# Two graph-attention layers and a binary layer: cross-partition maxima by transfers, last rows a window earlier, sign products one mix piece later, and a longer early tail

## The reference

```
def gat_layer(x, W, adj):
    Wh, Ws = split(x @ W, 2)
    a = softmax(Wh @ Ws.T) * adj
    return leaky_relu(a @ Wh + x, 0.01)

y = gat_layer(gat_layer(x, W_stack[0], adj), W_stack[1], adj)
x = layernorm(x + y)
xw = max(sign(x), 0) @ sign(weight).T
x = layernorm(x + relu(adj @ xw))
```

## Time and profile before

| | us |
|---|---|
| median of 3 runs (2173.22 to 2178.22) | 2175.34 |
| the profiled execution | 2172.28 |
| its span, first to last instruction | 2170.5 |
| TensorE busy | 2112.5 |
| VectorE, ScalarE, GpSimd busy | 1594.1, 908.4, 691.0 |
| granted TensorE clock, mean share | 0.996 |

### The profile page before, as it was taken

How to read it: one execution, slowest core, us unless ns; L and a number is a source line. 1 busy time by engine, 2 the same in 40 slices (tenths; PEclk the granted TensorE clock), 3 DMA queues, 4 the chain that set the end, 5 groups by cost and what they waited for, 6 DMA issues and landing times.

```text
span 2170.5 us, 38687 instructions
## 1 busy us (share of the span) xinstructions
PE 2112.5 (97%) x13260; PEld 1295.4 (60%) x13260; DVE 1594.1 (73%) x4051; ACT 908.4 (42%) x2043; POOL 691.0 (32%) x625
## 2 busy tenths in 40 slices
PE   6999999999999999999998999999999999999998
PEld 2446666666666666664445666666666666665444
DVE  7977877778777778777984676776677776766464
ACT  5764444434444444444764444344443444443000
POOL 2852223223223233323862332333323332332000
PEclk9999999999999999999999999999999999999999
DMA  7997878777877788779997978878978888779883
GB/s 217 213 216 153 174 156 169 146 158 153 165 151 167 153 164 158 160 149 231 213 215 143 186 157 167 169 159 170 173 155 163 169 169 173 159 147 236 237 275 118
DMA packets 779094, 380.11 MB, mean 175 GB/s; under 512 B 642576, under 2 KB 700944, under 8 KB 777232
## 3 DMA queue, kind: packets, MB, share of 16 engines
q1 hardware_dynamic: 768080, 341.82, 72.9%
q0 software_dynamic: 3328, 22.16, 6.9%
q10 hardware_dynamic: 7488, 13.63, 1.8%
HBM read 206.18 MB, written 59.11 MB: 122 GB/s over the span
## 4 chain that ended last, share of the span: by engine, by line
PE 85%; DVE 5%; issue 3%; DMA 3%; SPq 1%; ACT 1%; POOL 1%; DVEq 0%; POOLq 0%; ACTq 0%
PE banks L1120 35%; PE banks L1090 30%; PE banks L753 10%; PE banks L1615 6%; PE banks L1099 2%; DMA bits_t_a<-bits_a 1%; DMA adj_rows_a<-adj_rows 1%; PE banks L1079 1%; DVE halves_a L1345 1%; PE banks L584 1%; SPq L972 1%; POOL row_a L1281 0%; DVE acc_a L1367 0%; DVE work_a L1397 0%; DVE row_a L1300 0%
## 5 line engine op out<-in xcount | busy, mean ns | idle before, releaser
L1120 PE MATMUL banks<-values,probs_t_a 128*128 128x512 f16 x4056 | 959.1, 379 | 0.6 <-DVE acc_a L1367 0.6
L1281 POOL TENSOR_TENSOR row_a<-row_a,adj_rows_a 128x512 f32<-128x512 f32 (+1 forms) x364 | 456.7, 1269 | 1163.4 <-ACT row_a L1205 1126.0
L1120 PEld LDWEIGHTS banks<-values,probs_t_a 128*128 128x128 f16 x4056 | 397.1, 98 | 378.2 <-issue 2.4
L1090 PE MATMUL banks<-keys_t,q_even_a 128*128 128x256 f16 x3528 | 433.0, 273 | 12.8 <-ACT row_a L1197 10.2
L1345 DVE SCALAR_TENSOR_TENSOR halves_a<-row_a,halves_a 128x512 f16<-128x512 f32 (+1 forms) x364 | 277.5, 762 | 220.9 <-ACT halves_a L1220 218.3
L1197 ACT ACTIVATE row_a<-banks 128x256 f32<-128x256 f32 x468 | 177.3, 379 | 612.6 <-PE banks L1090 596.1
L1090 PEld LDWEIGHTS banks<-keys_t,q_even_a 128*128 128x128 f16 x3528 | 344.5, 98 | 114.5 <-ACT row_a L1197 9.3
L1090 PE MATMUL banks<-keys_t,q_odd_a 128*128 128x256 f16 x3024 | 370.0, 273 | 7.5 <-ACT row_a L1197 4.6
L1090 PEld LDWEIGHTS banks<-keys_t,q_odd_a 128*128 128x128 f16 x3024 | 294.1, 98 | 95.5 <-ACT row_a L1197 7.6
L1205 ACT ACTIVATE row_a<-row_a,shift_a,scales 128x512 f32<-128x512 f32 (+1 forms) x364 | 281.2, 774 | 161.7 <-DVE shift_a L1335 161.5
L1367 DVE SCALAR_TENSOR_TENSOR acc_a<-acc_a,factor_a,banks 128x512 f32<-128x512 f32 x312 | 232.8, 746 | 97.0 <-PE banks L1120 91.8
(11 more groups left out here) (130 smaller groups left out, 1479.2 us busy)
## 6 DMA issues: line engine op xcount, KB each, us to landing
adj_rows_a<-adj_rows SPq DMA_DIRECT2D x312, 256.0 KB, 3.2
adj_t<-adj_blocks POOLq DMA_DIRECT2D x104, 208.0 KB, 3.9
keys_t<-adj_t SPq DMA_DIRECT2D x26, 832.0 KB, 7.0
x_rows_a<-x_rows SPq DMA_DIRECT2D x52, 256.0 KB, 3.5
s_rows<-sum_rows_p SPq DMA_DIRECT2D x24, 512.0 KB, 3.1
values<-x_rows SPq DMA_DIRECT2D x13, 512.0 KB, 6.1
adj_rows_a<-adj_rows SPq DMA_DIRECT2D x52, 128.0 KB, 2.7
x_mid<-x_rows_a SPq DMA_DIRECT2D x26, 256.0 KB, 3.3
```

Source lines behind the costliest of these rows:

```text
L1090: last = pe.matmul(bank(w, name), queries(pair_of(w), q_block, qh, c), keys_t[:, kh, k_block, c, cols], start=(first and c == 0 and n == 0 ...
L1120: last = pe.matmul(out_bank(u), probs_t[:, turned_slot(w), u, ph * tiles + j, :], values[:, 4 * step_of(w) + j, vh, :], start=(j == 0 and ...
L1281: pool.tensor_tensor(piece, piece, adj_rows[:, n % ADJ_RING, 0:width(w)], ALU.mult).then_inc(masked, 1)
```

## The change

It has six parts. (1) `spread_w_peak` of layer 1's W is replaced by three functions: SP stores the 128 maxima to DRAM (`send_w_peak`), fetches them back broadcast to all partitions (`fetch_w_peaks`), and VectorE takes the maximum (`join_w_peaks`). The first all-reduce of W in layer 0 and those of the norms stay. (2) `spread_low_bits` becomes `gather_low_bits` on SP and a reduction in `note_low_bits`. (3) `last_rows` is cut into 16 parts of 3 matmuls, spread over windows 0 to 2 by a table. (4) Sign products stand behind mix (0,0), those of tiles 22 and 23 behind mix (1,1); `keep_product` stands behind the exponentials. (5) Six output banks, five early tiles. (6) In layer 0's start, W is scaled and split in two halves of columns, and the order of loads and turns is another.

```diff
-LAST_ROWS = 1
+LAST_ROWS = ((0, 1, 2, 3, 4), (4, 6, 7, 9, 10), (10, 12, 13, 15, 16))
-    LOADS_AHEAD = 8
+    LOADS_AHEAD = 11
...
+    def send_w_peak(sp):
+        sp.wait_ge(w_peak, layer + 1)
+        sp.dma_start(peak_row[:], facts[:, 0:1]).then_inc(w_peak_out, 16)
+    def fetch_w_peaks(sp):
+        sp.wait_ge(w_peak_out, 16)
...
+        sp.dma_start(w_peaks[:], peak_row.partition_broadcast(P)).then_inc(w_peak_in, 16)
+    def join_w_peaks(dve):
+        dve.wait_ge(w_peak_in, 16)
+        dve.reduce_max(facts[:, 1:2], w_peaks[:], AX_X).then_inc(w_peak_all, 1)
...
-    def last_rows(pe, t, side, part):
-        if part == 0:
+    def last_rows(pe, k):
+        t, side, c = T - 2 + k // 8, k // 4 % 2, k % 4
+        if c == 0:
             pe.wait_ge(turn_sem(t), landed_turn(t))
             pe.wait_ge(rows_copied, 4 * (first_pair + last_pair - 1 + side) if t == T - 2
                        else 4 * (first_pair + last_pair) + 1 + side)
...
     def sp_program(sp, turn_first_queries):       # project, layer 0
...
-            for i in range(1, LOADS_AHEAD):
+            load_x(sp, 1)
+            turn_x(sp, 0)
+            load_x(sp, 2)
+            turn_x(sp, 1)
+            for i in range(3, LOADS_AHEAD):
                 load_x(sp, i)
-            for t in range(RING):
-                turn_x(sp, t)
-                for i in range(LOADS_AHEAD + 2 * t, min(LOADS_AHEAD + 2 * t + 2, J)):
-                    load_x(sp, i)
+            turn_x(sp, 2)
+            for i in range(LOADS_AHEAD, J):
+                load_x(sp, i)
+            turn_x(sp, 3)
...
-            for c in range(DC):                   # act, layer 0
-                halve_w(c)
+            for side in (0, 1):
+                for c in range(DC):
+                    halve_w(c, cols_of(side))
...
             see_w(1)                              # dve, layer 0
-            x_lo_half(dve, 1)
             see_w(2)
             see_w(3)
             peak_of_pieces(dve)
+            x_lo_half(dve, 1)
             scale_w(dve)
-            for c in range(DC):
-                lo_w(c)
+            for side in (0, 1):
+                for c in range(DC):
+                    lo_w(c, side)
...
             for c in range(DC):                   # make_rows
-                if t == 0 and side == 0:
-                    pe.wait_ge(w_split, c + 1 if layer == 0 else DC + PIECES)
+                if t == 0 and layer == 0:
+                    pe.wait_ge(w_split, DC * side + c + 1)
+                elif t == 0 and side == 0:
+                    pe.wait_ge(w_split, 2 * DC + PIECES)
...
+            if ahead and piece_windows.get(w - 3, -1) == pieces - 1:      # attend, sp
+                ahead["send_w_peak"](sp)
+            if ahead and piece_windows.get(w - 5, -1) == pieces - 1:
+                ahead["fetch_w_peaks"](sp)
+            if last_layer and w == 5:
+                binary["gather_low_bits"](sp)
...
-            if LAST_ROWS <= w + LAG < LAST_ROWS + 2:                      # mix
-                now["last_rows"](pe, T - 2 + w + LAG - LAST_ROWS, u, piece)
+            if w + LAG < LAG:
+                for k in range(*LAST_ROWS[w + LAG][2 * u + piece:2 * u + piece + 2]):
+                    now["last_rows"](pe, k)
...
+            mix(w - LAG, 0, 0)                                            # attend, pe
             for t, u in made_now:
                 if t < binary["made_here"]:
                     pe.wait_ge(accumulated, through(w - LAG - 1, 1))
-                sign_product(pe, t)
-            mix(w - LAG, 0, 0)
+                    sign_product(pe, t)
...
             mix(w - LAG, 1, 1)
+            for t, u in made_now:
+                if t >= binary["made_here"]:
+                    sign_product(pe, t)
...
             copy_scores(w, 0)                                             # attend, act
-            for t, u in late_tiles(w, 7, 8) if last_layer else ():
-                keep_product(t)
             if 0 <= w - 1 < windows:
                 exps(w - 1)
+            if last_layer and w < windows:
+                for t, u in late_tiles(w, 7, 8):
+                    keep_product(t)
             copy_scores(w, 1)
...
-            if LAST_ROWS <= w < LAST_ROWS + 2:
-                now["copy_rows"](act, T - 2 + w - LAST_ROWS, 0)
+            if w == 2:
+                now["copy_rows"](act, T - 1, 0)
...
-            if LAST_ROWS <= w < LAST_ROWS + 2:
-                now["copy_rows"](act, T - 2 + w - LAST_ROWS, 1)
+            if w < LAG:
+                now["copy_rows"](act, T - 2 + w // 2, (w + 1) // 2)
...
+            if last_layer and w >= windows:
+                for t, u in late_tiles(w, 7, 8):
+                    keep_product(t)
...
-            if last_layer and w == 3:                                     # attend, pool
-                binary["spread_low_bits"](pool)
...
-            if ahead and piece_windows.get(w - 2, -1) == pieces - 1:
-                ahead["spread_w_peak"](pool)
...
-            if last_layer and w == 5:                                     # attend, dve
+            if last_layer and w == 8:
                 binary["note_low_bits"](dve)
...
-                if piece_windows.get(w - 3, -1) == pieces - 1:
+                if piece_windows.get(w - 7, -1) == pieces - 1:
+                    ahead["join_w_peaks"](dve)
                     ahead["scale_w"](dve)
...
-ADJ16_RING, OUT_RING, EARLY_TILES = 8, 4, 4
+ADJ16_RING, OUT_RING, EARLY_TILES = 8, 6, 5
...
+    def gather_low_bits(sp):
+        sp.wait_ge(low_bits_found, 1)
...
+        sp.dma_start(low_row[0:1], flag[:, 0:1]).then_inc(low_bits_gathered, 16)
     def note_low_bits(dve):
+        dve.wait_ge(low_bits_gathered, 16)
+        dve.reduce_max(flag[0:1, 1:2], low_row[0:1], AX_X).then_inc(low_bits_max, 1)
...
         for t in range(EARLY_TILES):                                      # binary, pe
             pe.wait_ge(adj16_loaded[t], 16)
+            if t == 4:
+                pe.wait_ge(accumulated, units)
             add_products(t, range(T - 2))
-            if t in (1, 2):
-                signs["sign_product"](pe, T - 3 + t)
+            if t in (2, 3):
+                signs["sign_product"](pe, T - 4 + t)
...
         for t in range(EARLY_TILES, T):
             pe.wait_ge(adj16_loaded[t % ADJ16_RING], 16 * (t // ADJ16_RING + 1))
-            pe.wait_ge(rows_done, t - OUT_RING + 1)
+            if t >= OUT_RING:
+                pe.wait_ge(rows_done, t - OUT_RING + 1)
```

More of the change, by code:

```diff
@@ L299, in project @@
     else:
+        peak_row, w_peak_out, w_peak_in = dram["peak_row"], sems["w_peak_out"], sems["w_peak_in"]
+        w_peaks = at(AT_PEAKS, f"w_peaks_p{layer}", [P, P], F32)
         w_piece = at(AT_W_PIECE, f"w_piece_p{layer}", [P, D], F32)
@@ L344, in spread_w_peak @@
         pool.partition_all_reduce(facts[:, 1:2], facts[:, 0:1], P, REDUCE_MAX).then_inc(w_peak_all, 1)
+    def send_w_peak(sp):
[3 more added lines that the diff above has]
+        sp.wait_ge(w_peak_out, 16)
+        for half in (HI, LO):
+            sp.wait_ge(keys_turned[half], 16 * layer * (J - 1))
+        sp.dma_start(w_peaks[:], peak_row.partition_broadcast(P)).then_inc(w_peak_in, 16)
+    def join_w_peaks(dve):
+        dve.wait_ge(w_peak_in, 16)
+        dve.reduce_max(facts[:, 1:2], w_peaks[:], AX_X).then_inc(w_peak_all, 1)
     def scale_w(dve):
@@ L425, in keys_made, with cols_of @@
         return kb[:, 0, 0:4] if i == last_pair else kb[:, i % 2, B11:]
+    def cols_of(side):
+        return slice(D, 2 * D) if side == 0 else slice(0, D)
     def row_bank(t, side):
@@ L580, in last_rows @@
                        else 4 * (first_pair + last_pair) + 1 + side)
-        cols = slice(D, 2 * D) if side == 0 else slice(0, D)
-        for c in range(part * DC // 2, (part + 1) * DC // 2):
-            for n, (xh, wh) in enumerate(((HI, HI), (HI, LO), (LO, HI))):
-                last = pe.matmul(row_bank(t, side), turned(t)[:, xh * DC + c, :], w16[:, wh, c, cols],
-                                 start=(c == 0 and n == 0), stop=(c == DC - 1 and n == 2))
-        if part == 1:
+        for n, (xh, wh) in enumerate(((HI, HI), (HI, LO), (LO, HI))):
+            last = pe.matmul(row_bank(t, side), turned(t)[:, xh * DC + c, :], w16[:, wh, c, cols_of(side)],
+                             start=(c == 0 and n == 0), stop=(c == DC - 1 and n == 2))
+        if c == DC - 1:
             last.then_inc(rows_made, 1)
@@ L1458, in dve_program @@
                 split(w - 1, 1)
-            if w == LAST_ROWS + 2:
+            if w == 3:
                 now["keys_lo_half"](dve, J - 1)
-            if w == LAST_ROWS + 3:
+            if w == 4:
                 now["values_lo_half"](dve, J - 1)
@@ L1543, in out_bank @@
     def out_bank(t):
-        return banks[:, (0, 1, 4, 5)[t % OUT_RING]]
+        return banks[:, (0, 1, 4, 5, 3, 7)[t % OUT_RING]]
     def scores_past(sp, step):
@@ L1571, in find_low_bits @@
```

(12 more changed lines are left out.)

44 lines of the change are left out of this document (24 added, 20 removed).

## The result

The changed kernel takes 2150.14 us in the median (2147.85 to 2151.33, 4 runs) against 2176.23 (2173.22 to 2178.22, 4 runs): a ratio of 0.9882, 95% interval 0.9868 to 0.9896, or 25.7 us (22.6 to 28.7). The forecast was 2148.2, from 27.1 us of gain.

A forecast was written before the change was run, and what follows sets the result against it. PE, busy 2112.5 of 2170.5 us, was taken as the bound, so only removing matmuls or idle PE time gains. Terms 13.7 + 5.2 + 2.6 + 5.6 + 0 = 27.1 us took the median from 2175.3 to 2148.2, range 2141 to 2157.

The forecast's parts named there:

- Low bits: Layer 1, window 3: without GpSimd's all-reduce its pause goes; 8.2 us gained, read from the offset between the layers.
- W's maxima: Layer 0, window 34: transfers replace GpSimd's all-reduce, its pause goes; 5.5 us gained, the added transfers costed at nothing.
- a pair with window 34 that stays long: Layer 0: pairs around window 34 should take 64.0 us on PE; if that pair stays long, the forecast is wrong.
- Last rows: Windows 0 to 2: four parts fit window 0's lost time; 2.6 us gained per layer, 5.2 for both, bounds 2.5 and 5.5.
- ScalarE's third copy: Window 1: ScalarE's third score copy stays ahead of PE by less than 1 us; otherwise half the 5.2 us gain goes.
- Sign products: Running windows: a mix piece in front removes PE's waits for `accumulate`; 2.6 us gained, bounds 1.5 and 3.
- D: Rival: `keep_product` frees the bank too late in 22 steps, 28.6 us lost, kernel ends at 2176.8; chance 0.03.
- Tail: Kernel's end: waits for bits and first output tile go, stall moves to last turned probabilities; 5.6 us gained, bounds 3 and 10.
- B: Rival, tail: last turned probabilities land after 4 us, 4 us more gain than forecast, 2144; chance 0.13.
- Start: Layer 0's start: first matmul moves from 20.55 to about 15.6, seventh tile stays near 54.8; costed at nothing.
- A: Rival, start: late x loads hold the norms and all behind them, costing 3 us, 2151; chance 0.17.
- C: Rival: GpSimd's pauses belong to something else and come back elsewhere, so the maxima's 13.7 us gain is absent, 2162; chance 0.05.

The follow-up runs named there:

- low bits alone: Kernel before with only layer 1's flag gathered by one small transfer instead of GpSimd's all-reduce: 2167.99 against 2177.24 us, ratio 0.9956.

## Why the prediction was right

The time came out 1.9 us above the forecast. The forecast for the profiled execution, 2145.2, was 6.1 us too low: the two profiled executions lie only 21.0 us apart, and the table has where the rest went, 3.83 us of it at the end of layer 0, which no term covered. Term by term, with the medians of the single parts and the stretches of the table:

- **Low bits**: forecast 8.2; 9.6 by medians, 8.2 by stretches. The offset between the two layers was the right measure.
- **W's maxima**: forecast 5.5; 3.5 by medians, 3.8 by stretches (3.1 shorter in the mean of the four kernels with both transfers as in the change and no more, 0.7 longer in the seven without). The pause is gone as predicted, and the term is too large by 1.7 to 2: windows 34 to 48, two pairs, take 129.9 us in the profile after, between the starts of their first exponentials, where 128.07 was named. The forecast's own sign of being wrong, a pair with window 34 that stays long, is there in part. The step that failed is "Added: three small transfers [...] I cost these at nothing". What was named behind them were the turns, and that they wait for VectorE; the danger foreseen was a result that lands late. The results were in time: VectorE read the maxima at 514.53 without a wait. It was the transfers behind that were held: one issue took 4.30 us instead of 1.23, and an adjacency load was late.
- **Last rows**: forecast 5.2; 5.7 by medians and 5.2 by stretches. Window 0 still ended at VectorE's read, and the full 2.59 us a layer say that ScalarE's third copy did not come too late.
- **Sign products**: forecast 2.6 in the running windows; 5.0 by stretches. The profile of before had 2.2 us of these waits in 4 places, the others without the part 2.8 to 5.2 us in 5 or 6, so that one profile was a low base for this term. For the tail's part, a loss of 1.2, the medians with it give 2.0 in all where 1.4 was forecast. `keep_product` releases PE nowhere: D is out.
- **Tail**: forecast 6.8 without the turned probabilities; 7.6 by medians and 6.8 by the table. With them 5.6 was forecast, and the two profiles of the kernel after have 4.9 and 5.1. In the kernel after the stall moved to the last probabilities as predicted, 3.44 us and 0.77 for 3.8, and the slow stretch behind was 4.37 us for 12 matmuls, where 2.75 is usual: 1.6 us of loss where 1.2 stood. B is out: the transfer was not fast. The answer to it, loads that stand ahead "in both versions", was what could be changed: 3.8 us.
- **Start**: forecast 0; the seventh tile at 54.81 says 0, the medians a cost of 0 to 3 us. PE waits before the third tile as well (1.76 us), which was not foreseen and doesn't count, for the same reason. A, late x loads, is not what the trace shows: VectorE's last square begins at 32.28 (before 32.21). If there is a cost, its place isn't found. The chain that sets the seventh tile has an idle stretch of 6.94 us behind an all-reduce as well, that of the norms; whether it would go with a transfer was not tried.
- C is out by the low bits alone: they gained all of their term.

The mechanisms were mostly right, but that the sum came within 1.9 us was partly luck: the errors went both ways (W's maxima, perhaps the start, and the end of layer 0 below the forecast, the sign products above), and the sum was nearer than its terms.

## What to carry to other kernels

A reduction over partitions on GpSimd amid elementwise work is not priced by its 0.4 us: GpSimd idled about 7 us on each side, and its next products came 8.3 us late. Two of them in a row cost hardly more than one. Where it is replaced by transfers, look at what stands behind them: the gather of 128 numbers of 4 bytes into one row of SBUF cost nothing that could be seen, while behind most stores of such a column to DRAM a later issue took over 4 us. That the destination makes the difference is likely, but the two were not tried at one place. A transfer that the end waits for goes ahead of large loads that have time (3.8 us here). And moving the first matmul forward by 4.7 us was worth nothing, since the place where PE next waits is set by another chain.

## What was not expected of the hardware

- A store of 0.5 KB to DRAM as 128 pieces of 4 bytes took 7.6 to 9.9 us to land, amid other traffic, on SyncE's queue and on ScalarE's alike; the gather of as many bytes into SBUF 2.0 to 2.8 us. Behind seven of nine such stores in one kernel a later issue took 4.6 to 9.5 us and ended 11 to 14 us after the store.
- Behind the same wait of 1.3 us at the same place the granted clock stayed at 1.00 in five profiled executions and fell to 0.50, the lower level of 1.2 GHz, in two others: 1.67 us for 18 matmuls.
